# Hybrid Mamba-2 / feed-forward chain on one core: the sum over 1024 channels of the mixers' squares moves from TensorE (column-tiled products) to GpSimd (three additions)

## Chip, cores and metric

One Trainium2 chip, one NeuronCore of it. The metric is device time in microseconds (us) of one execution of the whole kernel, as the median of several runs. Everything is float32 (a few operands are rounded to fp32r). PE is TensorE, DVE is VectorE, ACT is ScalarE, POOL is GpSimd, SP is the sync engine, which here only issues DMAs.

## The reference, cut to what matters

Four layers one after the other over x of shape (4, 1024, 512): mixer A, feed-forward, mixer B, the same feed-forward again, each as x = x + layer(layernorm(x)). Both mixers are state-space mixers of width 1024: they project the token, convolve it, run the recurrence over time, and end with a gated normalisation over the 1024 channels:

```
mixer A:  yf  = y * silu(gate)
          var = mean(yf * yf, axis=-1)
          out = (norm_w * (yf * rsqrt(var + EPS))) @ out_proj_w.T
mixer B:  var = mean(square(y), axis=-1)
          out = ((y * rsqrt(var + EPS)) * norm_w * silu(z)) @ out_proj_w
```

What the change touches is the mean of the squares over the 1024 channels of each token.

## The kernel before

The 4096 tokens go through each mixer in 16 supertiles of 256 tokens, each of two tiles of 128 tokens (j = 0 and 1). Supertile 0, the last two and the 13 between them (a hardware loop) have the same body. The work of a supertile is software-pipelined: while supertile i is in its recurrence, TensorE projects supertile i+1 into the gaps ("fill"). The order on every engine is written out by hand, and semaphores connect the engines.

TensorE runs the list that `schedule(prev, nxt)` gives. Names of it that the text uses:

- `zza`, `zzb`, `z0a`, `z0b`, `z1`, `z2`, `blk..`, `dt`: projections of fill, line 655 (`dt` is line 684);
- `xT0..3`, `BT`/`GT` (`BG` in mixer A): transposes and small products at the head of a supertile;
- `yoffJa`, `yoffJb`: state times C, two banks for tile J (lines 725 and 727); `from_state` on DVE (line 1221) multiplies each by the decay into y1, in two halves, and GpSimd adds `skip` to y1 (line 1441);
- `segJ.p`: exponents of the decay matrices, from which ACT makes `decay` (lines 936 and 943) and DVE multiplies it by the masked product (`slot_mult`, line 1232) for the `ydiag` products;
- `rs0` and `prs` (line 746): the squares of a tile, summed. `rs0` is that of tile j=0, in the middle of its own supertile; `prs` is that of tile j=1, in the head of the next supertile;
- `rt0` and `prt` (line 750), then `out0` and `pout` (line 756): the turned column of sums, and the output product of the tile, which waits in TensorE's order behind `rt0`/`prt`;
- `small1` (line 716) follows `pout` by two uses; it takes over the PSUM bank of `pout`, which DVE's `out_add` (line 1277) has to have read.

All steps except `seg`, `ydiag`, `ident` and `xT` are "uses" of two PSUM banks in turn (`work`): a use may start when the use two before it has been read out (`freed`). With `rs0` and `prs` in the list, `yoff1a` takes the bank of `z0b`, `yoff1b` that of `rs0`, `rt0` that of `yoff1a`, and `out0` that of `yoff1b`.

The squares: DVE's `gate` (line 1257) writes yz = y * silu(z) in two halves; ACT's `square` (line 953) writes `sq`, [128 channels, 8 blocks, 128 tokens], in two halves. Mixer B squares y itself. `rs0`/`prs` multiplies each of the eight blocks by 32 columns of ones; block b goes to the column group b mod 4 of the array, so that four run side by side, and the bank then holds four partial sums, each repeated over 32 partitions. DVE copies it to `rs` (`square_sums`, line 1263), and `rt0`/`prt` multiplies `rs` by `quad_row`, which picks one partition of each group and adds them with the token turned to the partition. DVE makes the variance of it (line 1267), ACT its logarithm and exponential, DVE one Newton step, and `out_add` scales the output product and adds the residual.

DVE's order in the second half of a supertile of mixer B is: last state addition, `gate` of tile 0, the six multiply-adds of the last two convolution blocks (line 1111), `square_sums`, `from_state(1)`, `rms_var`, `slot_mult` of tile 1. In mixer A the convolution lies before the gate. In the head it is: masked product (1182), `make_xdt(0)` (1160 in B in two halves, 1165 in A), `square_sums`, `from_state(0)`, `rms_var`, `make_xdt(1)`, `slot_mult(0, 0)`, Newton step, `slot_mult(0, 1)`, `out_add`.

GpSimd's order of a tile (`tile_steps`) is: the second right side of the exponents (line 1406, B only), e (1421, j=0 only), `skip` (1435), y1 + skip (1441), xw (1448 in B in two halves, 1452 in A), state decay (1458).

Of the kernel before, what the change touches and what calls it, by code (L numbers as in the profile page):

```python
# [8 lines left out]
ALU = mybir.AluOpType  # L9
ACT = mybir.ActivationFunctionType  # L10

P = 128
# [16 lines left out]
FREE = 2  # L29
# [168 lines left out]
def build_constants(nc, ctx, ffn_w, mixers, weights, arena, mixer_signals, x_src):  # L198
# [18 lines left out]

    c["quad_row"] = sb("quad_row", [P, 1])
    hd = sb("hd", [P, 2, 4, 16])
# [13 lines left out]
    with nc.Block() as block:  # L233
# [44 lines left out]
        @block.vector  # L278
        def _(dve):
            dve.wait_ge(made, c["steps"])  # L280
            nc.vector.tensor_reduce(c["of_head"][:], hd[:].rearrange("p o e c -> p (o e) c"), mybir.AxisListType.X, ALU.add).then_inc(built, 1)
            nc.vector.tensor_reduce(c["low_row"][:], low[:].rearrange("p a b -> p (a b)"), mybir.AxisListType.X, ALU.add
                                    ).then_inc(built, 1)
            nc.vector.tensor_reduce(c["l_row"][:], lrow[:].rearrange("p a b -> p (a b)"), mybir.AxisListType.X, ALU.add
                                    ).then_inc(built, 1)
            nc.vector.tensor_reduce(c["quad_row"][:], c["ident"][:].rearrange("p (q e) -> p e q", e=32)[:, 0:1, :],
                                    mybir.AxisListType.X, ALU.add).then_inc(built, 1)
            dve.wait_ge(built, 4)
            nc.vector.tensor_scalar(c["sign_row"][:], c["low_row"][:], -2.0, 1.0, ALU.mult, ALU.add).then_inc(built, 1)
            nc.vector.tensor_scalar(c["s_row"][:], c["l_row"][:], -1.0, 1.0, ALU.mult, ALU.add).then_inc(built, 1)  # L290
            dve.wait_ge(built, 6)
            count = [6]
# [10 lines left out]
def mixer_phase(nc, sig, before, cfg, c, arena, later, psum, x_src, x_dst, w):  # L303
# [21 lines left out]
    with ctx:  # L325
# [100 lines left out]
        sq_done = sig("sq_done")  # L426
        rs_ready = sig("rs_ready")
        rv_ready = sig("rv_ready")
        r1_ready = sig("r1_ready")
# [20 lines left out]
        def head(prev, nxt):  # L450
            return (["zza", "xT0", "xT1", "xT2", "xT3"] + b_and_g + ["zzb"]
                    + (["prs"] if prev else []) + ["yoff0a", "yoff0b", "seg0.0"] + (["prt"] if prev else [])
                    + (["xnT0"] if nxt else []) + (["pout"] if prev else []) + (["xnT1"] if nxt else [])
                    + ["ident0", "small1"])

        def schedule(prev, nxt):
# [9 lines left out]
            steps += ["z0a", "z0b"] if nxt else []  # L466
            steps += ["rs0", "yoff1a", "yoff1b", "seg1.0", "rt0", "out0"]
            for p in range(NP):
# [29 lines left out]
        pro_steps = ["xnT0", "xnT1", "dt"] + blocks + ["z0a", "z0b", "z1", "z2", "sums", "small0"]  # L498
        epi_steps = ["prs", "prt", "pout"]
        first_uses, loop_uses, last_uses = ([s for s in schedule(*a) if is_use(s)]  # L500
# [43 lines left out]
        def freed(eng, name, i, n):  # L544
# [27 lines left out]
            elif name[:5] == "state":  # L572
                eng.wait_ge(state_ready, FREE + i * 4 + 2 * int(name[5]) + (2 if FOLD else "ab".index(name[6]) + 1))
            elif name in ("rs0", "prs"):
                eng.wait_ge(rs_ready, FREE + i * 2 + (name == "rs0"))
            elif name in ("rt0", "prt"):
                eng.wait_ge(rv_ready, FREE + i * 2 + (name == "rt0"))
            elif name in ("out0", "pout"):
                eng.wait_ge(out_done, FREE + i * 2 + (name == "out0"))
            else:  # L580
                raise ValueError(name)

        with nc.Block() as block:
# [68 lines left out]
            def _(pe):  # L652
# [12 lines left out]
                def use(name, sec):  # L665
# [63 lines left out]
                    elif name[:5] == "state":  # L729
# [11 lines left out]
                    elif name in ("rs0", "prs"):  # L741

                        pe.wait_ge(sq_done, FREE + 2 * (2 * i + (name == "rs0")))
                        for b in range(KE):
                            q = b % 4
                            mm = nc.tensor.matmul(bank[32 * q:32 * q + 32, 0:P], ones[:, 0:32], sq[:, b, :],
                                                  start=(b < 4), stop=(b >= 4))
                    elif name in ("rt0", "prt"):
                        pe.wait_ge(rs_ready, FREE + 2 * i + (name == "rt0"))
                        mm = nc.tensor.matmul(bank[:, 0:1], rs[:], c["quad_row"][:], start=True, stop=True)  # L750
                    else:
# [310 lines left out]
            def _(dve):  # L1062
# [197 lines left out]

                def square_sums(sec, name):
                    dve.wait_ge(work_full, sec.full(name))
                    nc.vector.tensor_copy(rs[:], sec.bank(name)[:, 0:P]).then_inc(rs_ready, 1)

# [23 lines left out]
                def supertile(sec, prev, nxt):  # L1288
                    i = sec.i
                    masked_gt(sec)  # L1290
                    make_xdt(sec, 0)
                    if prev:
                        square_sums(sec, "prs")
                    from_state(sec, 0)
# [31 lines left out]
                    square_sums(sec, "rs0")  # L1326
                    from_state(sec, 1)
# [25 lines left out]
                for s in (xn_ready, raw_ready, conv_done, halo_done, xdt_done, hilo_ready, y1_ready, state_ready,  # L1353
                          yz_done, out_done, rs_ready, rv_ready, m_ready):
                    dve.sem_inc(s, FREE)
# [38 lines left out]
                sec = epilogue()  # L1394
                square_sums(sec, "prs")
                rms_var(sec, "prt")
# [5 lines left out]
            def _(pool):  # L1402
# [10 lines left out]

                def tile_steps(i, j, ln=None):
                    tile = 2 * i + j
# [3 lines left out]
                    if j == 0:  # L1419
# [5 lines left out]
                        if FOLD:  # L1425

                            pool.wait_ge(dec_done, FREE + tile)
                            for q in range(2):
# [3 lines left out]
                            ins.then_inc(folded, 1)  # L1432
                            pool.wait_ge(folded, FREE + i + 1)
                    pool.wait_ge(xt_ready, FREE + 4 * i + 2 * j + 2)
                    nc.gpsimd.tensor_tensor(skip[:].rearrange("p (h q) -> p h q", h=H),
                                            xt[:, j, :].rearrange("p (h q) -> p h q", h=H),
                                            d_skip[:].unsqueeze(2).to_broadcast([P, H, HP]), ALU.mult
                                            ).then_inc(skip_done, 1)
                    pool.wait_ge(y1_ready, FREE + 2 * tile + 2)
                    pool.wait_ge(skip_done, FREE + tile + 1)  # L1440
# [22 lines left out]

                for s in (skip_done, y1x_ready, dec_done, kept, xw_ready, folded):
# [3 lines left out]
                tile_steps(0, 0)  # L1468
                tile_steps(0, 1, ln=2)
# [3 lines left out]
                for i in (NSUP - 2, NSUP - 1):  # L1473
                    tile_steps(i, 0)
                    tile_steps(i, 1)

def ffn_phase(nc, sig, before, tag, c, arena, following, psum, x_src, x_dst, w):
# [647 lines left out]
```

## Time and profile before

| | |
|---|---|
| median of 3 runs | 2862.99 us (2861.88 to 2865.03) |
| span of the profiled execution | 2859.7 us |
| granted TensorE clock, mean | 0.980 of full speed |
| PE busy | 2733.3 us, 96% |
| DVE busy | 2009.9 us, 70% |
| ACT busy | 1527.0 us, 53% |
| POOL busy | 926.1 us, 32% |
| supertile of mixer A | about 66.5 us |
| supertile of mixer B | about 78.7 us |

The profiled execution's own time is its span; the median of the runs lies 3.3 us (0.1%) above it. Times in rows are microseconds from the start of the span. A row of the timeline gives start, length, engine, line, operation, what is written and read; "x2" is a merged pair, and what stands in brackets is how long the engine sat idle before it and what ended that. Each float32 matrix product shows as two records.

### The profile page before, as it was taken

Reading aid. Unit: us, or ns where it says so; the run is one execution under the profiler, and the core shown is the slowest. Engines: PE = TensorE matmul, PEld = TensorE weight load, DVE = VectorE, ACT = ScalarE, POOL = GpSimd, SP = SyncE. Lnnn points to the kernel's source line nnn. Section 1 sums busy time; section 2 is a strip of 40 time slices with the busy share of each in tenths; the row PEclk is TensorE's granted clock in tenths of the full one; section 3 lists DMA queues with packets and bytes.
Section 4 is the critical chain, followed back from the end, with each engine's and each line's share of the span. In section 5 each row is a group of like instructions: output and inputs, shape, how many; then the busy total and the mean of one; then the engine's idle time right before and its main releaser. Section 6 shows DMA issues by size and latency. Waiting matters only on the chain. (4 is left out here: it accounts for less than half of the span.)

```text
span 2859.7 us, 49906 instructions
## 1 busy us (share of the span) xinstructions
PE 2733.3 (96%) x17464; PEld 1845.0 (65%) x17464; DVE 2009.9 (70%) x3695; ACT 1527.0 (53%) x2418; POOL 926.1 (32%) x614
## 2 busy tenths in 40 slices
PE   7999999999999999996899999999999999997996
PEld 6777766777766665455666666666666666664453
DVE  5666666666666663377788888888888888885267
ACT  3444444445455442341577666766667776665242
POOL 2222223222223321232233444333333334332134
PEclk9999999999999999998999999999999999998998
DMA  4000000000000034145000000000000000022333
GB/s 125 23 23 22 22 22 22 23 28 29 22 22 22 16 121 152 45 147 204 12 23 22 22 22 16 21 22 22 15 15 22 22 22 22 15 95 89 112 118 133
DMA packets 79935, 139.59 MB, mean 49 GB/s; under 512 B 17896, under 2 KB 17896, under 8 KB 78832
## 3 DMA queue, kind: packets, MB, share of 16 engines
q1 hardware_dynamic: 70752, 125.92, 12.9%
q10 hardware_dynamic: 9104, 12.63, 1.4%
q8 instruction: 48, 0.79, 0.1%
q14 instruction: 31, 0.25, 0.0%
HBM read 104.98 MB, written 33.55 MB: 48 GB/s over the span
## 5 line engine op out<-in xcount | busy, mean ns | idle before, releaser
L655 PE MATMUL work<-b_xnT,shared_w 128*128 128x256 f32 x2304 | 545.8, 388 | 1.8 <-DVE b_parts L1192 1.3
L655 PE MATMUL work<-a_xnT,shared_w 128*128 128x256 f32 x2176 | 509.4, 392 | 1.3
L655 PEld LDWEIGHTS work<-b_xnT,shared_w 128*128 128x128 f32 x2304 | 426.1, 191 | 90.6 <-issue 30.1
L655 PEld LDWEIGHTS work<-a_xnT,shared_w 128*128 128x128 f32 x2176 | 419.0, 195 | 73.8 <-issue 12.3
L1232 DVE TENSOR_TENSOR b_decay<-b_decay,b_gt 128x1024 f32<-128x1024 f32 x256 | 351.7, 1395 | 119.3 <-ACT b_decay L943 115.8
L936 ACT ACTIVATE b_decay<-seg 128x1024 f32<-128x1024 f32 x256 | 248.5, 1029 | 112.0 <-PE seg L781 111.8
L943 ACT ACTIVATE b_decay<-b_decay 128x1024 f32<-128x1024 f32 x256 | 266.1, 1073 | 0.0
L1406 POOL TENSOR_TENSOR b_rhs<-b_l_side,of_head 128x1024 fp32r<-128x1024 f32 x32 | 82.0, 2563 | 552.4 <-DVE b_l_side L1201 552.4
L1441 POOL TENSOR_TENSOR a_y<-a_y,a_skip 128x1024 f32<-128x1024 f32 x32 | 90.9, 2840 | 484.1 <-DVE a_y L1221 484.1
L1111 DVE SCALAR_TENSOR_TENSOR shared_cv<-shared_pre,a_conv_w,shared_cv 128x256 f32<-128x256 f32 x432 | 189.7, 482 | 74.6 <-ACT shared_cv L880 68.9
L1111 DVE SCALAR_TENSOR_TENSOR shared_cv<-shared_pre,b_conv_w,shared_cv 128x256 f32<-128x256 f32 x480 | 232.1, 517 | 14.2 <-ACT shared_cv L880 6.3
L756 PE MATMUL work<-a_w_out,a_yz 128*128 128x512 f32 x512 | 229.0, 600 | 2.3 <-DVE a_y L1221 0.5
L756 PE MATMUL work<-b_w_out,b_yz 128*128 128x512 f32 x512 | 226.8, 596 | 0.6
L879 ACT COPY shared_pre<-work 128x256 f32<-128x256 f32 x304 | 114.7, 377 | 201.4 <-PE work L655 201.2
L886 ACT COPY shared_z<-work 128x256 f32<-128x256 f32 (+1 forms) x192 | 85.8, 447 | 253.3 <-PE work L655 252.4
L1232 DVE TENSOR_TENSOR a_decay<-a_decay,a_gt 128x1024 f32<-128x1024 f32 x64 | 136.5, 2152 | 84.9 <-ACT a_decay L943 84.4
L756 PEld LDWEIGHTS work<-a_w_out,a_yz 128*128 128x128 f32 x512 | 95.5, 192 | 112.2 <-issue 108.5
L756 PEld LDWEIGHTS work<-b_w_out,b_yz 128*128 128x128 f32 x512 | 94.7, 190 | 109.1 <-issue 107.1
L795 PE MATMUL y<-b_decay,b_xdt 128*32 128x128 f32 x4096 | 142.8, 280 | 5.8 <-DVE b_decay L1232 5.7
L795 PEld LDWEIGHTS y<-b_decay,b_xdt 128*32 128x32 f32 x4096 | 105.6, 111 | 61.7 <-issue 50.8
L1441 POOL TENSOR_TENSOR b_y<-b_y,b_skip 128x1024 f32<-128x1024 f32 x32 | 82.9, 2591 | 130.6 <-DVE b_y L1221 130.6
L1653 PE MATMUL y<-f_x1T,shared_pre 128*128 128x512 f32 x256 | 122.9, 610 | 0.0
(314 smaller groups left out, 4612.4 us busy)
## 6 DMA issues: line engine op xcount, KB each, us to landing
shared_x<-in_L_attn_a_x SPq DMA_DIRECT2D x16, 512.0 KB, 3.5
a_x_res<-in_L_attn_a_x SPq DMA_DIRECT2D x32, 256.0 KB, 2.6
x_mid<-a_x_res SPq DMA_DIRECT2D x32, 256.0 KB, 2.1
shared_w<-in_L_ffn_d_w SPq DMA_DIRECT2D x2, 4096.0 KB, 14.0
f_d_w<-in_L_ffn_d_w SPq DMA_DIRECT2D x2, 4096.0 KB, 14.5
f_x_res<-x_mid SPq DMA_DIRECT2D x8, 1024.0 KB, 5.9
f_bc_w<-x_mid SPq DMA_DIRECT2D x8, 1024.0 KB, 5.6
shared_x<-x_mid SPq DMA_DIRECT2D x16, 512.0 KB, 3.6
```

What stands on the lines that cost most here:

```text
L655: mm = nc.tensor.matmul(dst, w_in[:, k, col:col + m], xnT[:, k, :], start=(k == 0), stop=(k == KD - 1))
L756: mm = nc.tensor.matmul(bank[:, :], yz[:, k, :], w_out[:, k, :], start=(k == 0), stop=(k == KE - 1))
L795: mm = nc.tensor.matmul(ybank[32 * q:32 * q + 32, slot * P:(slot + 1) * P], xdt[:, j, 4 * slot + q, 16 * odd:16 * odd + 32], decay[:, slot ...
L879: nc.scalar.copy(pre[0:m, b, HALO:], bank[0:m, 0:SUP])
L886: nc.scalar.copy(z_raw[:, got[0]:got[-1] + 1, :], sec.bank(name)[:, 0:len(got) * SUP].rearrange("p (b t) -> p b t", t=SUP)).then_inc(z_rea ...
L936: nc.scalar.activation(decay[:, slot_buffer(j, s)].rearrange("p h l -> p (h l)"), seg[s % 2][:, :], ACT.Relu, scale=-1.0).then_inc(seg_tak ...
L943: nc.scalar.activation(d, d, ACT.Exp, scale=-1.0).then_inc(exp_done, 1)
L1111: ins = nc.vector.scalar_tensor_tensor(out=cv[0:m, b, :], in0=pre[0:m, b, t:t + SUP], scalar=conv_w[0:m, b, t:t + 1], in1=cv[0:m, b, :], o ...
L1232: nc.vector.tensor_tensor(d, d, gt[:, j].unsqueeze(1).to_broadcast([P, 8, P]), ALU.mult).then_inc(m_ready, 1)
L1406: nc.gpsimd.tensor_tensor(rhs[1][:], l_side[:, 1].unsqueeze(1).to_broadcast([P, 8, P]), c["of_head"][:].unsqueeze(2).to_broadcast([P, 8, P ...
L1441: nc.gpsimd.tensor_tensor(y1[:], y1[:], skip[:], ALU.add).then_inc(y1x_ready, 1)
L1653: mm = nc.tensor.matmul(ybank[:, (m % 2) * 512:(m % 2 + 1) * 512], gate_w[:, k, m * P:(m + 1) * P], x1T[n][:, k, :], start=(k == 0), stop= ...
```

## The change

`rs0` and `prs` leave TensorE's list and with them two of the uses of the `work` banks; DVE's copy and `quad_row` go. GpSimd adds the eight blocks of `sq` in place: 512 columns, 256 columns, then 128 columns into `rs`. `rt0`/`prt` multiplies `rs` (now [128 channels, 128 tokens]) by one column of ones. On GpSimd the sums of the previous tile stand ahead of `skip` when j=0 (after e), and after `skip` and ahead of y1 + skip when j=1; those of the very last tile stand at the end.

```
-                    + (["prs"] if prev else []) + ["yoff0a", "yoff0b", "seg0.0"] + (["prt"] if prev else [])
+                    + ["yoff0a", "yoff0b", "seg0.0"] + (["prt"] if prev else [])
...
-            steps += ["rs0", "yoff1a", "yoff1b", "seg1.0", "rt0", "out0"]
+            steps += ["yoff1a", "yoff1b", "seg1.0", "rt0", "out0"]
...
-                    elif name in ("rs0", "prs"):
-
-                        pe.wait_ge(sq_done, FREE + 2 * (2 * i + (name == "rs0")))
-                        for b in range(KE):
-                            q = b % 4
-                            mm = nc.tensor.matmul(bank[32 * q:32 * q + 32, 0:P], ones[:, 0:32], sq[:, b, :],
-                                                  start=(b < 4), stop=(b >= 4))
                     elif name in ("rt0", "prt"):
                         pe.wait_ge(rs_ready, FREE + 2 * i + (name == "rt0"))
-                        mm = nc.tensor.matmul(bank[:, 0:1], rs[:], c["quad_row"][:], start=True, stop=True)
+                        mm = nc.tensor.matmul(bank[:, 0:1], rs[:], ones[:, 0:1], start=True, stop=True)
...
-                def square_sums(sec, name):
-                    dve.wait_ge(work_full, sec.full(name))
-                    nc.vector.tensor_copy(rs[:], sec.bank(name)[:, 0:P]).then_inc(rs_ready, 1)
...
+                def square_sums(tile):
+
+                    pool.wait_ge(sq_done, FREE + 2 * tile + 2)
+                    nc.gpsimd.tensor_tensor(sq[:, 0:4, :], sq[:, 0:4, :], sq[:, 4:8, :], ALU.add).then_inc(sq_halved, 1)
+                    pool.wait_ge(sq_halved, FREE + tile + 1)
+                    nc.gpsimd.tensor_tensor(sq[:, 0:2, :], sq[:, 0:2, :], sq[:, 2:4, :], ALU.add).then_inc(sq_quartered, 1)
+                    pool.wait_ge(sq_quartered, FREE + tile + 1)
+                    pool.wait_ge(rv_ready, FREE + tile)
+                    nc.gpsimd.tensor_tensor(rs[:], sq[:, 0, :], sq[:, 1, :], ALU.add).then_inc(rs_ready, 1)
...
+                    if j == 0 and sums_before:
+                        square_sums(tile - 1)
                     pool.wait_ge(xt_ready, FREE + 4 * i + 2 * j + 2)
...
+                    if j == 1:
+                        square_sums(tile - 1)
                     pool.wait_ge(y1_ready, FREE + 2 * tile + 2)
```

## Rows read from the trace of the kernel before

**Rows 1.** The page: its span line and the engines' busy time.

```profile
span 2859.7 us, 49906 instructions
...
PE 2733.3 (96%) x17464; PEld 1845.0 (65%) x17464; DVE 2009.9 (70%) x3695; ACT 1527.0 (53%) x2418; POOL 926.1 (32%) x614
```

**Rows 2.** Groups by line and form: busy us, mean ns, idle before.

```profile
L746 PE MATMUL work<-a_sq,ones 128*32 128x128 f32 x512 | 20.6, 279 | 3.8 <-ACT a_sq L953 3.8
L746 PE MATMUL work<-b_sq,ones 128*32 128x128 f32 x512 | 20.6, 279 | 5.7 <-ACT b_sq L953 5.7
```

**Rows 3.** One line's instructions each: min/median/max ns.

```profile
L1441 POOL TENSOR_TENSOR b_y<-b_y,b_skip x32: 2350/2366/2919, 1382.2 to 2596.9; 128x1024 f32<-128x1024 f32 x32
...
L2027 POOL TENSOR_TENSOR f_bc_w<-f_bc_w,f_out_beta_row x32: 1259/1267/1297, 1203.3 to 2850.9; 128x512 f32<-128x512 f32 x32
...
L1111 DVE SCALAR_TENSOR_TENSOR shared_cv<-shared_pre,b_conv_w,shared_cv x480: 470/482/1619, 1346.6 to 2528.3; 128x256 f32<-128x256 f32 x160
```

**Rows 4.** Timeline of mixer B around rs0, all engines.

```profile
2051.14 1.93 POOL L1435 TENSOR_TENSOR b_skip<-b_xt,b_d_skip 128x1024 f32<-128x1024 f32 x1
2051.25 1.19 ACT L953 ACTIVATE b_sq<-y 128x512 f32<-128x512 f32 x2 [2.90 <-DVE b_yz L1257]
2051.74 3.84 DVE L1111 SCALAR_TENSOR_TENSOR shared_cv<-shared_pre,b_conv_w,shared_cv 128x256 f32<-128x256 f32 x6
...
2054.12 0.65 PE L746 MATMUL work<-b_sq,ones 128*32 128x128 f32 x16
...
2054.70 2.27 PE L727 MATMUL work<-b_state,b_bcs 128*128 128x512 f32 x4
2055.50 0.28 DVE L1263 COPY b_rs<-work 128x128 f32<-128x128 f32 x1
...
2057.00 0.69 DVE L1221 TENSOR_TENSOR b_y<-work,b_e 128x512 f32<-128x512 f32 x1 [0.45 <-PE work L727]
...
2057.74 7.13 PE L756 MATMUL work<-b_w_out,b_yz 128*128 128x512 f32 x16
```

**Rows 5.** Timeline of mixer B, GpSimd and DVE at once.

```profile
2061.20 2.05 POOL L1448 TENSOR_TENSOR b_xw<-b_xdt,b_e 128x512 f32<-128x512 f32 x1
2060.35 1.97 DVE L1232 TENSOR_TENSOR b_decay<-b_decay,b_gt 128x1024 f32<-128x1024 f32 x1 [2.44 <-ACT b_decay L943]
```

**Rows 6.** Timeline of the head of a supertile of mixer B.

```profile
2007.95 1.09 ACT L953 ACTIVATE b_sq<-y 128x512 f32<-128x512 f32 x2
...
2008.34 1.94 POOL L1435 TENSOR_TENSOR b_skip<-b_xt,b_d_skip 128x1024 f32<-128x1024 f32 x1 [0.17 <-POOL b_e L1421]
2008.59 2.83 DVE L1160 TENSOR_TENSOR b_xdt<-b_xt,b_dt 128x512 f32<-128x512 f32 x2
...
2013.17 0.38 PE L750 MATMUL work<-quad_row,b_rs 128*128 128x1 f32 x2
...
2021.22 0.75 DVE L1277 SCALAR_TENSOR_TENSOR b_x_res<-work,b_rr,b_x_res 128x512 f32<-128x512 f32 x1
...
2022.33 0.61 PE L716 MATMUL work<-tri_le,b_aa 128*128 128x128 f32 x4
```

**Rows 7.** Timeline of mixer A: its head, then around rs0.

```profile
787.18 1.15 ACT L953 ACTIVATE a_sq<-a_yz 128x512 f32<-128x512 f32 x2
...
791.25 0.38 PE L750 MATMUL work<-quad_row,a_rs 128*128 128x1 f32 x2
...
800.85 0.44 PE L716 MATMUL work<-tri_le,a_aa 128*64 128x128 f32 x4 [0.15 <-DVE a_x_res L1277]
...
823.38 1.23 ACT L953 ACTIVATE a_sq<-a_yz 128x512 f32<-128x512 f32 x2 [3.69 <-DVE a_yz L1257]
...
828.23 7.13 PE L756 MATMUL work<-a_w_out,a_yz 128*128 128x512 f32 x16
```

**Rows 8.** Timeline of the end of mixer B.

```profile
2619.07 1.19 ACT L953 ACTIVATE b_sq<-y 128x512 f32<-128x512 f32 x2 [3.28 <-DVE b_yz L1257]
...
2621.55 0.35 PE L750 MATMUL work<-quad_row,b_rs 128*128 128x1 f32 x2 [0.49 <-DVE b_rs L1263]
```

More of the change, by code:

```diff
@@ L216, in build_constants @@
     c["keep"] = sb("keep", [P, NSUP + 1])
-    c["quad_row"] = sb("quad_row", [P, 1])
     hd = sb("hd", [P, 2, 4, 16])
@@ L285, in _ @@
                                     ).then_inc(built, 1)
-            nc.vector.tensor_reduce(c["quad_row"][:], c["ident"][:].rearrange("p (q e) -> p e q", e=32)[:, 0:1, :],
-                                    mybir.AxisListType.X, ALU.add).then_inc(built, 1)
-            dve.wait_ge(built, 4)
+            dve.wait_ge(built, 3)
             nc.vector.tensor_scalar(c["sign_row"][:], c["low_row"][:], -2.0, 1.0, ALU.mult, ALU.add).then_inc(built, 1)
             nc.vector.tensor_scalar(c["s_row"][:], c["l_row"][:], -1.0, 1.0, ALU.mult, ALU.add).then_inc(built, 1)
-            dve.wait_ge(built, 6)
-            count = [6]
+            dve.wait_ge(built, 5)
+            count = [5]
             def link(ins):
@@ L427, in mixer_phase @@
         rs_ready = sig("rs_ready")
+        sq_halved, sq_quartered = sig("sq_halved"), sig("sq_quartered")
         rv_ready = sig("rv_ready")
@@ L498, in mixer_phase @@
         pro_steps = ["xnT0", "xnT1", "dt"] + blocks + ["z0a", "z0b", "z1", "z2", "sums", "small0"]
-        epi_steps = ["prs", "prt", "pout"]
+        epi_steps = ["prt", "pout"]
         first_uses, loop_uses, last_uses = ([s for s in schedule(*a) if is_use(s)]
@@ L573, in freed @@
                 eng.wait_ge(state_ready, FREE + i * 4 + 2 * int(name[5]) + (2 if FOLD else "ab".index(name[6]) + 1))
-            elif name in ("rs0", "prs"):
-                eng.wait_ge(rs_ready, FREE + i * 2 + (name == "rs0"))
             elif name in ("rt0", "prt"):
@@ L740, in use @@
                                                   start=True, stop=True)
-                    elif name in ("rs0", "prs"):
-                        pe.wait_ge(sq_done, FREE + 2 * (2 * i + (name == "rs0")))
-                        for b in range(KE):
-                            q = b % 4
-                            mm = nc.tensor.matmul(bank[32 * q:32 * q + 32, 0:P], ones[:, 0:32], sq[:, b, :],
-                                                  start=(b < 4), stop=(b >= 4))
                     elif name in ("rt0", "prt"):
                         pe.wait_ge(rs_ready, FREE + 2 * i + (name == "rt0"))
-                        mm = nc.tensor.matmul(bank[:, 0:1], rs[:], c["quad_row"][:], start=True, stop=True)
+                        mm = nc.tensor.matmul(bank[:, 0:1], rs[:], ones[:, 0:1], start=True, stop=True)
                     else:
@@ L1291, in supertile @@
                     make_xdt(sec, 0)
-                    if prev:
-                        square_sums(sec, "prs")
                     from_state(sec, 0)
@@ L1325, in supertile @@
                         gate(sec, 0)
-                    square_sums(sec, "rs0")
                     from_state(sec, 1)
@@ L1353, in _ @@
                 for s in (xn_ready, raw_ready, conv_done, halo_done, xdt_done, hilo_ready, y1_ready, state_ready,
-                          yz_done, out_done, rs_ready, rv_ready, m_ready):
+                          yz_done, out_done, rv_ready, m_ready):
                     dve.sem_inc(s, FREE)
@@ L1394, in _ @@
                 sec = epilogue()
-                square_sums(sec, "prs")
                 rms_var(sec, "prt")
@@ L1412, in norm_rsqrt, with tile_steps @@
                     nc.gpsimd.tensor_tensor(ln_r[:], ln_v[:], c["root"][:], ALU.pow).then_inc(r0_ready, 1)
-                def tile_steps(i, j, ln=None):
+                def square_sums(tile):
[6 more added lines that the diff above has]
+                    nc.gpsimd.tensor_tensor(rs[:], sq[:, 0, :], sq[:, 1, :], ALU.add).then_inc(rs_ready, 1)
+                def tile_steps(i, j, ln=None, sums_before=True):
                     tile = 2 * i + j
@@ L1462, in tile_steps @@
                         norm_rsqrt(ln)
-                for s in (skip_done, y1x_ready, dec_done, kept, xw_ready, folded):
+                for s in (skip_done, y1x_ready, dec_done, kept, xw_ready, folded, rs_ready, sq_halved, sq_quartered):
                     pool.sem_inc(s, FREE)
@@ L1467, in _ @@
                 pool.wait_ge(small_loaded, 16 * 5)
-                tile_steps(0, 0)
+                tile_steps(0, 0, sums_before=False)
                 tile_steps(0, 1, ln=2)
@@ L1475, in _ @@
                     tile_steps(i, 1)
+                square_sums(2 * NSUP - 1)
 def ffn_phase(nc, sig, before, tag, c, arena, following, psum, x_src, x_dst, w):
```

## Prediction, made before the changed kernel was run

> **What bounds the kernel now.** I read the page first. PE is busy 96% of the span, DVE 70%, POOL 32% [rows 1]; the reader is to see that TensorE sets the pace and that GpSimd looks free. Next the groups by line: the work that leaves TensorE is 20.6 us in each mixer, 41.2 us in all, 1.4% of the span [rows 2]. A share says nothing of where a wait ends, so the rest comes from the timeline around the four places at which a tile's sum is made: `prs` in the head and `rs0` in the middle, in mixer A and in mixer B. There the question is what releases `out0`, and what releases `small1` after `pout`, since TensorE is dense behind both and a shift of either moves the whole supertile. In the middle of mixer B DVE is already the late one: the squares are summed by 2054.77, but DVE's copy starts only at 2055.50, when its six convolution steps are through; the second half of y1 ends at 2057.69 and `out0` starts at 2057.74 [rows 4]. In the head, `small1` starts at 2022.33 in mixer B, behind an `out_add` that ended at 2021.97 [rows 6], and at 800.85 in mixer A, where it waited for `out_add` [rows 7]. So DVE is the second bound, close behind, at three of the four places.
>
> **Price of the three sums.** GpSimd's add of two full tiles takes 2350 ns for 1024 columns and 1259 ns for 512 [rows 3]: (2350 - 1259) / 512 = 2.13 ns a column on a base of 0.17 us. So 512, 256 and 128 columns take 1.26, 0.71 and 0.44 us, 2.41 us; with about 0.08 us for each hand-over, `rs` is there 2.65 us after the squares if nothing is in the way. Columns 256 and 128 are not in the trace; below they are bounded by nothing and by one 512-column add each (3.8 us in all).
>
> **What they cost DVE.** In the head of mixer B, two halves of xdt take 2.83 us beside a `skip` of 1.94 us [rows 6], and one half alone takes about 0.68 us in the same line's shortest case, so DVE stood for nearly the whole of `skip`. In the middle, six convolution steps take 3.84 us, with `skip` on until 2053.07, where six at 0.42 us of spacing need 2.5 us [rows 4]; one such step is 470 ns alone and up to 1619 [rows 3]. The other way round, xw at 2061.20 takes 2.05 us, double its need, because the decay product that started at 2060.35 runs to 2062.32; and when that ends the waiting GpSimd goes first [rows 5]. I read this as: a DVE instruction that reads two tiles of SBUF and a GpSimd instruction exclude each other, and they take turns. What reads PSUM on DVE (`from_state`, the gate, `out_add`) isn't held up (0.69 us each time [rows 4]). Of a GpSimd instruction all but some 0.15 us at each end holds, so three sums hold about 2.41 - 0.45 = 1.95 us.
>
> The Trainium skill says the same of the pair (page "SBUF — State Buffer", section "SBUF: two separate sides"): it is an exclusive lock, kept for the whole instruction, and the other fully blocks; the trace agrees with [rows 5]. A sharing of bandwidth would leave most of the 1.95 us to DVE, and by it the change would come out as the first rival below.
>
> **Middle of mixer B (15 supertiles with convolution behind the gate).** Removed: `rs0` (0.65 us of PE) and the copy (0.28 us of DVE). Squares end at 2052.44, `skip` at 2053.07 [rows 4]. The sums then take turns with the convolution steps (first sum up to about 2054.5, then a step, second to 2055.4, a step, third to 2056.2), and the six steps end near 2055.5 + 1.95 = 2057.5 instead of 2055.5. Then two halves of y1, 1.29 us: 2058.8. `out0` needs the bank of `yoff1b`, so it starts at about 2058.85 instead of 2057.74: **+1.1 us**. `rt0` waits for the first half (2058.2), not for `rs`. Behind: y1 + skip on GpSimd is 1.1 us late too, and has 5 us before `ident1`. Bounds: if GpSimd lets the convolution run through first, sums lie from 2055.5 to 2058.0 and `out0` goes at 2058.5 (+0.75); if the sums hold DVE for all of 2.65 us, +1.8. I take +1.1, as the turns in [rows 5] give it. Sum 15 x 1.1 = 16.5.
>
> **Head of mixer B (15).** Squares end at 2009.04 [rows 6]. One half of xdt(0) gets between the sums, so `rs` comes at 2012.0 to 2012.3 and `prt` at about 2012.3, 0.85 us earlier than 2013.17. But `skip` now stands behind the sums: it runs from 2012.3 to 2014.2, where DVE wants xdt(1) from 2012.9. In turns: half of xdt(1) to 2014.8, y1 + skip to 2017.0, the other half to 2017.6, half of xw to 2018.5, `slot_mult(0,0)` to 2019.7, half of xw to 2020.6, `slot_mult(0,1)` to 2021.7, `out_add` to 2022.4 instead of 2021.97. `small1` then starts near 2022.6 instead of 2022.33: **+0.3**. TensorE's gain at `prt` is lost at `small1`. Bounds: -0.8 (no blocking, everything follows `prt`) and +0.9 (one more turn lost). ACT isn't moved: its table load and gate function stand before the exponentials. 15 x 0.3 = 4.5.
>
> **Head of mixer A (15).** Squares end at 788.33; xdt(0) on DVE (1.2 us, from 787.66) holds the first sum until 788.87; `rs` at 791.3, `prt` at 791.35 against 791.25 [rows 7], so no gain. `skip` again moves behind the sums, to 793.2, and xdt(1), which ran at 791.77 with nothing beside it, waits for it. In the same turns `out_add` ends at 801.3 instead of 800.80, and `small1`, at 800.85 already released by it [rows 7], follows: **+0.5**, bounds -0.2 and +0.9. 15 x 0.5 = 7.5.
>
> **Middle of mixer A (15).** The convolution is done before the gate, so nothing on DVE takes turns. Squares end at 824.61 [rows 7], `rs` comes at 827.3, `rt0` at 827.35, `out0` 0.49 us later at 827.85 instead of 828.23: **-0.4**, bounds -0.6 (the y1 halves decide, 827.6) and +0.75 (sums of 3.8 us). 15 x -0.4 = -6.
>
> **Ends.** Behind the last tile nothing covers the chain. From the end of the squares at 2620.26 to `prt` at 2621.55 are 1.29 us [rows 8]; with the sums 2.65, so +1.4 in each mixer, +2.8. `quad_row` is one small reduction ahead of everything: nothing. The waits that are added stand on GpSimd; what is queued behind them is `skip` in the head, priced above, and y1 + skip in the middle. No DMA is issued or moved; the SP queue's store of x_res only follows `out_add`.
>
> Sum: 16.5 + 4.5 + 7.5 - 6 + 2.8 = +25.3 us on the profiled execution's 2859.7 us, 2885 us. The median of the runs lies 3.3 us above that execution, so **2888 us**, 0.9% slower.
>
> **Rivals.** (1) *Hidden, faster.* The sums don't hold DVE. Then `out0` in the middle of B goes at 2056.9 (-0.85), the head of B gains 0.8, A's head 0.15 and middle 0.4: 15 x 2.2 = 33 less 2.8 gives about **2833 us**. For it: GpSimd is idle two thirds of the time and TensorE is the bound [rows 1]. Against it: xdt and convolution beside `skip`. It decides once the sums take less than about 0.8 us from DVE in the middle of B.
> (2) *The two sides cancel.* TensorE's savings are the size of DVE's losses: `small1` is held up nowhere in B (gain 0.8 instead of 0.3 lost), the rest as forecast: 25.3 - 16.5 = +9, and with -0.2 in A's head 0: about **2863 us**.
> (3) *Worse cascade.* Each head loses a further turn (+0.9 twice) and the middle of B 1.8 us, A's middle gains nothing: 15 x 3.6 + 2.8 = +57: **2920 us**. For it: the exchange at the lock in [rows 5] is read from few cases.
> Beside (1): TensorE's array changes its grouping for `rs0` and back. The Trainium skill (page "TensorEngine Tiling (Array Packing)", section "Tiling Modes") says that such a change drains TensorE; no row here shows the drain by itself, and it would come back at both ends of each removed step.
>
> **How the numbers follow.** Forecast 0.66, of which nothing ends below 2869; (1) 0.13, (2) 0.11, (3) 0.10. What this kernel's measurement can tell from no change is about 0.2%, 5.7 us. Faster 0.15 (all of (1), a little of (2)); same 0.08; slower 0.77. The likeliest case has 2873 to 2905 for itself: 2859.7 + 3.3 plus the sum with the middle of B at its low bound of +0.75 and the heads at 0 (+10), and with each head a little over half way to its upper bound (+42). The range 2858 to 2918 leaves out (1) and the upper half of (3).
>
> **What the profile after would show.** Right: six convolution steps behind the gate of B take about 4.4 to 5.8 us; the wait of TensorE before `rt0`/`out0` in B is ended by DVE's y1, and `out0` starts about 6.4 us after the end of the squares (5.3 before); xdt(1) in the heads starts later than `prt` and is long; line 750 waits for GpSimd's `rs` in A. Supertile of B +1.4 us, of A +0.1 us. Wrong: conv steps at 470 ns beside the sums; a supertile of B shorter than before; GpSimd's adds of 256 and 128 columns above 1 us each, which would turn A's middle into a loss. The weakest step is the order in which the two engines get the lock, and with it both heads.

## The result and the profile after

The changed kernel takes 2878.65 us (median of 4 runs, 2876.51 to 2879.03) where the kernel before takes 2863.17 us (4 runs, 2861.88 to 2865.03): a ratio of 1.0052, 95% interval 1.0038 to 1.0066. It is 0.5% slower. The direction is as forecast; the size is 9 us below the 2888 us of the forecast.

The page of the changed kernel, its span and busy line and three groups (busy us, mean ns; idle before them and its releaser):

```profile
span 2877.3 us, 47876 instructions
...
PE 2700.9 (94%) x16440; PEld 1830.6 (64%) x16440; DVE 2054.4 (71%) x3630; ACT 1527.0 (53%) x2418; POOL 1095.4 (38%) x806
...
L1100 DVE SCALAR_TENSOR_TENSOR shared_cv<-shared_pre,b_conv_w,shared_cv 128x256 f32<-128x256 f32 x480 | 255.4, 565 | 14.2 <-ACT shared_cv L869 6.3
L745 PE MATMUL work<-b_w_out,b_yz 128*128 128x512 f32 x512 | 240.7, 626 | 3.2 <-DVE b_y L1210 3.2
```

TensorE has 32 us less to do than in [rows 1] and the span is 17.6 us longer. GpSimd took on 169 us. DVE lost 64 copies (18 us) and is still 44 us busier. Work that the diff doesn't touch takes longer: the convolution of mixer B 23 us (517 ns a step before, 565 after), xdt 23 us and the decay products 15 us over both mixers. The output products of B are untouched too, and their mean is 626 ns instead of 596.

The three sums by line (min/median/max ns, first and last start):

```profile
L1399 POOL TENSOR_TENSOR a_sq<-a_sq x32: 1262/1266/1596, 93.1 to 1085.0; 128x512 f32<-128x512 f32 x32
...
L1399 POOL TENSOR_TENSOR b_sq<-b_sq x32: 1258/1442/1692, 1420.8 to 2633.2; 128x512 f32<-128x512 f32 x32
...
L1401 POOL TENSOR_TENSOR a_sq<-a_sq x32: 722/727/740, 94.4 to 1086.3; 128x256 f32<-128x256 f32 x32
...
L1404 POOL TENSOR_TENSOR a_rs<-a_sq x32: 453/458/462, 95.2 to 1087.1; 128x128 f32<-128x128 f32 x32
```

At their shortest they cost 1.26, 0.72 and 0.45 us, as worked out from [rows 3]. In mixer B the median of the first is 0.18 us more: in the middle of B it runs beside the convolution.

The middle of mixer B, timeline of all engines (the supertile of [rows 4], 7.55 us later):

```profile
2058.50 1.93 POOL L1429 TENSOR_TENSOR b_skip<-b_xt,b_d_skip 128x1024 f32<-128x1024 f32 x1
2058.61 1.20 ACT L942 ACTIVATE b_sq<-y 128x512 f32<-128x512 f32 x2 [2.90 <-DVE b_yz L1246]
2059.10 5.39 DVE L1100 SCALAR_TENSOR_TENSOR shared_cv<-shared_pre,b_conv_w,shared_cv 128x256 f32<-128x256 f32 x6
...
2060.39 1.45 POOL L1399 TENSOR_TENSOR b_sq<-b_sq 128x512 f32<-128x512 f32 x1
...
2060.64 1.48 DVE L1100 SCALAR_TENSOR_TENSOR shared_cv<-shared_pre,b_conv_w,shared_cv 128x256 f32<-128x256 f32 x1
...
2061.92 0.78 POOL L1401 TENSOR_TENSOR b_sq<-b_sq 128x256 f32<-128x256 f32 x1
...
2062.16 0.83 DVE L1100 SCALAR_TENSOR_TENSOR shared_cv<-shared_pre,b_conv_w,shared_cv 128x256 f32<-128x256 f32 x1
...
2062.78 0.52 POOL L1404 TENSOR_TENSOR b_rs<-b_sq 128x128 f32<-128x128 f32 x1
...
2062.91 0.67 DVE L1100 SCALAR_TENSOR_TENSOR shared_cv<-shared_pre,b_conv_w,shared_cv 128x256 f32<-128x256 f32 x1
...
2064.41 1.28 DVE L1210 TENSOR_TENSOR b_y<-work,b_e 128x512 f32<-128x512 f32 x2
...
2065.15 0.38 PE L739 MATMUL work<-ones,b_rs 128*128 128x1 f32 x2 [1.45 <-DVE b_y L1210]
...
2065.74 7.13 PE L745 MATMUL work<-b_w_out,b_yz 128*128 128x512 f32 x16 [0.22 <-DVE b_y L1210]
```

Six convolution steps take 5.39 us instead of 3.84 us. The three rows of single steps (x1) are the second, third and fourth of the six, each from a narrower window of the same timeline. The three sums end at 2061.84, 2062.70 and 2063.30, and these steps end at 2062.12, 2062.99 and 2063.58: each step that met a sum ends 0.28 to 0.29 us behind it, whatever its own start, where a step alone takes 0.48 us. That is what turns give. If the two only shared a bandwidth, a slowed step could also end ahead of the sum beside it, and none does. `rs` is complete at 2063.30, but `rt0` starts at 2065.15, behind the first half of y1 on DVE, and `out0` behind the second half. TensorE stands for 1.45 + 0.22 us: `rs0`, which used to fill 0.65 us of this stretch, is gone, and DVE is later.

The head of mixer B, the same supertile (against [rows 6]):

```profile
2019.58 1.94 POOL L1429 TENSOR_TENSOR b_skip<-b_xt,b_d_skip 128x1024 f32<-128x1024 f32 x1
2019.73 0.38 PE L739 MATMUL work<-ones,b_rs 128*128 128x1 f32 x2
2020.24 4.59 DVE L1149 TENSOR_TENSOR b_xdt<-b_xt,b_dt 128x512 f32<-128x512 f32 x2
...
2028.80 0.74 DVE L1263 SCALAR_TENSOR_TENSOR b_x_res<-work,b_rr,b_x_res 128x512 f32<-128x512 f32 x1
2029.59 0.71 PE L712 MATMUL work<-tri_le,b_aa 128*128 128x128 f32 x4 [0.54 <-DVE b_x_res L1263]
```

Mixer A, head and then middle of one supertile (against [rows 7], 3.75 us earlier):

```profile
787.64 1.90 POOL L1429 TENSOR_TENSOR a_skip<-a_xt,a_d_skip 128x1024 f32<-128x1024 f32 x1
787.73 0.38 PE L739 MATMUL work<-ones,a_rs 128*128 128x1 f32 x2 [0.68 <-POOL a_rs L1404]
...
797.48 0.44 PE L712 MATMUL work<-tri_le,a_aa 128*64 128x128 f32 x4 [0.68 <-DVE a_x_res L1263]
...
823.46 0.46 POOL L1404 TENSOR_TENSOR a_rs<-a_sq 128x128 f32<-128x128 f32 x1
...
824.28 7.13 PE L745 MATMUL work<-a_w_out,a_yz 128*128 128x512 f32 x16
```

In both heads `skip` stands behind the sums, xdt(1) is long (4.59 us for its two halves in B, 3.46 us before), and `small1` waits for `out_add`. In the middle of A nothing is lost.

**Where the 17.6 us are.** From the starts of successive supertiles (the activation of xs) in both traces. Mixer A: 15 periods average 66.48 us before and 66.04 after. Behind a shorter first one they come in two lengths, 65.79 and 67.47 before (7 each), 65.6 (9) and 67.27 (5) after. Mixer B: 78.6 to 79.0 before, most of them 78.65, but for a last one of 79.85; after, nine of 79.1 and six of 80.8 to 81.0, mean 79.80. So a usual supertile of A is 0.2 us shorter, one of B 0.46 us longer; besides, 1.7 us come and go by the piece, six times more in B and two times fewer in A. Up to the last store of A the changed kernel is 2.8 us ahead (loop -6.6, its last supertile with the epilogue +3.5, the start the rest). B costs 20.2 us (loop +15.8, last supertile +4.4).

**The piece of 1.7 us.** Windows of 4 us of the changed kernel: a short supertile of A, a long one of A, a long one of B (length; PE, PEld, DVE, ACT, POOL busy with instructions; granted clock; DMA share, GB/s):

```profile
133.00:137.00 4.00, 3.34 (x31) 2.93 (x30) 2.49 (x4) 0.59 (x1) 3.81 (x3) 1.00 0.17 66
137.00:141.00 4.00, 4.00 (x21) 3.54 (x21) 1.14 (x6) 1.55 (x5) 0.00 (x0) 1.00 0.22 66
...
264.00:268.00 4.00, 3.33 (x32) 2.92 (x30) 2.66 (x4) 0.59 (x1) 3.92 (x3) 1.00 0.17 66
268.00:272.00 4.00, 4.00 (x15) 3.30 (x15) 1.14 (x6) 1.13 (x4) 0.07 (x1) 0.62 0.24 66
...
1742.00:1746.00 4.00, 2.34 (x11) 0.91 (x9) 3.90 (x8) 2.22 (x4) 1.35 (x3) 1.00 0.00 0
1746.00:1750.00 4.00, 4.00 (x6) 1.77 (x7) 3.13 (x2) 2.08 (x4) 3.93 (x2) 0.62 0.00 0
```

One window of the kernel before, in a long supertile of A:

```profile
203.00:207.00 4.00, 4.00 (x12) 3.21 (x12) 0.89 (x5) 1.30 (x4) 0.00 (x0) 0.57 0.28 66
```

PE's timeline in that supertile of B:

```profile
1745.36 0.38 PE L739 MATMUL work<-ones,b_rs 128*128 128x1 f32 x2 [1.44 <-DVE b_y L1210]
...
1745.96 8.83 PE L745 MATMUL work<-b_w_out,b_yz 128*128 128x512 f32 x16 [0.21 <-DVE b_y L1210]
```

After a stand of 1.44 + 0.21 us the clock is granted at 0.62 of full speed over 4 us, most of that time at the lower of its two levels (1.2 instead of 2.4 GHz), and `out0` takes 8.83 us instead of 7.13. The stretch at the lower level lasts 3.4 us (granted 0.50 from 1746.94 to 1750.35), and half of it is the 1.7 us. The same stand at 2065 left it at 7.13 us. In A the fall comes just behind `small1`, in 5 of 15 supertiles; the two shown have the same busy time of PE ahead of it to 0.01 us (3.34 and 3.33), and one falls. The kernel before had it too, in 7 supertiles of A at the same place (0.57 in the window above; that supertile began at 179.05), with a stand of 0.15 us there [rows 7]; I had averaged over it as "about 66.5 us". There the falls come in every second supertile, 133.1 us apart. The first supertile of each mixer, whose work isn't dense yet, has a stretch at the lower level in every kernel here, the one before too; the counts leave it out.

The end of mixer B, timeline (against [rows 8]):

```profile
2631.87 1.30 ACT L942 ACTIVATE b_sq<-y 128x512 f32<-128x512 f32 x2 [3.94 <-DVE b_yz L1246]
...
2635.98 0.56 PE L739 MATMUL work<-ones,b_rs 128*128 128x1 f32 x2 [4.22 <-POOL b_rs L1404]
2636.40 9.51 PE L745 MATMUL work<-b_w_out,b_yz 128*128 128x512 f32 x16
```

TensorE stands for 4.22 us where [rows 8] show 0.49, because `prs` no longer breaks the wait, and then does `pout` in 9.51 us instead of 7.11 (in A 8.81 instead of 7.11).

### The profile page after: what moved, and what is told of

The parts are those of the page before. It is cut to its first block and busy times, and to the rows that moved or that the text cites. A ratio compares the mean times of both kernels' runs of the same rounds, so it can differ in the third digit from the quotient of the medians.

```text
span 2877.3 us, 47876 instructions
## 1 busy us (share of the span) xinstructions
PE 2700.9 (94%) x16440; PEld 1830.6 (64%) x16440; DVE 2054.4 (71%) x3630; ACT 1527.0 (53%) x2418; POOL 1095.4 (38%) x806
## 5 line engine op out<-in xcount | busy, mean ns | idle before, releaser
L1221 DVE TENSOR_TENSOR b_decay<-b_decay,b_gt 128x1024 f32<-128x1024 f32 x256 | 361.3, 1433 | 94.8 <-ACT b_decay L932 91.4
L1100 DVE SCALAR_TENSOR_TENSOR shared_cv<-shared_pre,b_conv_w,shared_cv 128x256 f32<-128x256 f32 x480 | 255.4, 565 | 14.2 <-ACT shared_cv L869 6.3
L745 PE MATMUL work<-b_w_out,b_yz 128*128 128x512 f32 x512 | 240.7, 626 | 3.2 <-DVE b_y L1210 3.2
L1399 POOL TENSOR_TENSOR a_sq<-a_sq 128x512 f32<-128x512 f32 x32 | 45.1, 1409 | 487.2 <-ACT a_sq L942 487.2
L1394 POOL TENSOR_TENSOR ln_r<-ln_v,root 128x2 f32<-128x2 f32 x30 | 34.3, 1142 | 235.6 <-DVE ln_v L1065 235.6
```

What stands on the lines that cost most here:

```text
L745: mm = nc.tensor.matmul(bank[:, :], yz[:, k, :], w_out[:, k, :], start=(k == 0), stop=(k == KE - 1))
L1100: ins = nc.vector.scalar_tensor_tensor(out=cv[0:m, b, :], in0=pre[0:m, b, t:t + SUP], scalar=conv_w[0:m, b, t:t + 1], in1=cv[0:m, b, :], o ...
L1221: nc.vector.tensor_tensor(d, d, gt[:, j].unsqueeze(1).to_broadcast([P, 8, P]), ALU.mult).then_inc(m_ready, 1)
L1399: nc.gpsimd.tensor_tensor(sq[:, 0:4, :], sq[:, 0:4, :], sq[:, 4:8, :], ALU.add).then_inc(sq_halved, 1)
```

## The experiments

Each ran beside the kernel before on the same chip (its median 2863 to 2864.5 us).

**Sums that nobody uses.** The kernel before, with the three adds put into GpSimd's order at the change's places, into a spare tile. TensorE's and DVE's work stay as they were; ACT's next squares wait for the third add as well, and in the trace it was never the wait that held them (they waited for the gate alone).

```diff
+def ghost_sums(tile):        # gh is a spare tile
+    pool.wait_ge(sq_done, FREE + 2 * tile + 2)
+    nc.gpsimd.tensor_tensor(gh[:, 0:4, :], sq[:, 0:4, :], sq[:, 4:8, :], ALU.add).then_inc(gh_a, 1)
...
+                    if j == 0 and sums_before:
+                        ghost_sums(tile - 1)
...
+                    if j == 1:
+                        ghost_sums(tile - 1)
```

> The kernel before, with the three additions on GpSimd added at the places where the change has them, but into a spare tile that nobody on the path reads (only the next tile's squares wait for them). TensorE and DVE do all that they did. Theory L (the additions cost by excluding DVE's two-input instructions): the six convolution steps behind the gate of mixer B take about 5.4 us instead of 3.84, out0 in B is about 1.3 us later, both heads lose 0 to 0.4 us, so 2863 + 20 to 35 us. Rival W (the loss of the changed kernel is the longer wait of TensorE for rs, and GpSimd's additions disturb nobody): 2863 us within 3, convolution 3.84 us.

Measured 2900.54 us, ratio 1.0129 (1.0112 to 1.0146). The expected range of theory L ended at 2898. Its timeline in the middle of B:

```profile
2074.31 5.41 DVE L1114 SCALAR_TENSOR_TENSOR shared_cv<-shared_pre,b_conv_w,shared_cv 128x256 f32<-128x256 f32 x6
2075.61 1.45 POOL L1419 TENSOR_TENSOR b_gh<-b_sq 128x512 f32<-128x512 f32 x1
...
2079.98 1.13 PE L729 MATMUL work<-b_state,b_bcs 128*128 128x512 f32 x2 [1.58 <-DVE b_rs L1266]
```

The adds alone, feeding nothing, stretch the six steps from 3.84 to 5.41 us and cost 37 us. About 8.5 us of that are the clock: five long supertiles more at 1.7 us each (nine long supertiles in A instead of seven, three in B instead of none). A usual supertile of A is 0.3 us longer, one of B 1.36 us. In B the loss is larger than in the changed kernel because DVE's copy, behind the stretched steps, now holds up `yoff1b`: TensorE stands 1.58 us for it. GpSimd's work isn't free although GpSimd has time; the changed kernel, which has the same adds and does without the products and the copy, is 22 us faster than this one.

The Trainium skill says so of the pair (page "SBUF — State Buffer", section "SBUF: two separate sides"): a GpSimd instruction and a DVE instruction with two inputs in SBUF exclude each other, and whichever is first holds the other off for the whole instruction. The trace agrees: 5.41 us here, and the ends of the single steps in the changed kernel.

**One sum instead of three.** The changed kernel with the 128-column add only; blocks 2 to 7 are left out of the variance.

```diff
-nc.gpsimd.tensor_tensor(sq[:, 0:4, :], sq[:, 0:4, :], sq[:, 4:8, :], ALU.add).then_inc(sq_halved, 1)
...
-nc.gpsimd.tensor_tensor(sq[:, 0:2, :], sq[:, 0:2, :], sq[:, 2:4, :], ALU.add).then_inc(sq_quartered, 1)
```

> The changed kernel with one addition of 128 columns instead of three (0.46 us of GpSimd instead of 2.45; blocks 2 to 7 are left out of the variance). Theory L: the convolution group is back near 4.2 us, TensorE's wait before rt0 in mixer B falls under 0.4 us, with it the phases at half clock in out0, and the saved column-tiled products show: about 2835 us. Rival (the gain isn't there in any case, because TensorE's removed steps were hidden behind DVE): 2855 to 2865 us.

Measured 2829.94 us, ratio 0.9886 (0.9869 to 0.9902). Nearly every period of A is 64.69 us, nearly every one of B 78.48; the six steps take 4.05 us, and TensorE no longer waits ahead of `rt0`. So the first two sums cost 49 us, and what the change removes is worth 33 us if most of the sums is gone. Both figures have the clock in them: one long supertile in A (seven before, five in the changed kernel) and two in B (none and six). The kernel comes within 4 us of the first rival's 2833 us, which had no term for the clock, so that nearness is in part luck.

**Work in TensorE's hole.** The changed kernel, with six products nobody uses behind `seg1.0` in B, once the squares are there.

```diff
+if name == "rt0" and cfg.tag == "b":
+    pe.wait_ge(yz_done, FREE + 2 * (2 * sec.i + 1))
+    pe.wait_ge(sq_done, FREE + 2 * (2 * sec.i + 1))
+    keep_running(nc, ybank, ident, 6)
```

> The changed kernel with six unused 128x128 float32 products (1.3 us) on TensorE in mixer B just ahead of rt0, where it waits 1.45 us for DVE's y1. Theory C (in 6 of 15 supertiles of B the wait lets the granted clock fall and out0 then takes 8.8 instead of 7.1 us): all supertiles of B take 79.1 us, none 80.8, and the kernel 2878.6 - 10 = about 2868 us. Rival (the longer supertiles come from something else, or the products only delay rt0): same or up to 5 us slower.

Measured 2864.75 us, ratio 1.0005 (0.9996 to 1.0015). PE's timeline:

```profile
2056.79 1.60 PE L54 MATMUL y<-ident 128*128 128x128 f32 x12
...
2058.92 7.13 PE L745 MATMUL work<-b_w_out,b_yz 128*128 128x512 f32 x16 [0.21 <-DVE b_y L1214]
```

`out0` starts no earlier, yet B's periods are all 79.1 to 79.4 us and the kernel is 13.9 us faster than the changed one: 10.1 us in B's loop and 3.3 in its last supertile with the epilogue. A, where nothing was filled, kept its five falls. That is the clock's share of the loss.

**Mixer A alone.** The change in A, mixer B as before.

```diff
+NEW = cfg.tag in "a"      # selects the form of every part of the change
```

> The change in mixer A alone; mixer B keeps its column-tiled sums on TensorE. By the two profiles mixer A had become 2.8 us shorter up to its last store and mixer B 20.2 us longer, so 2863 - 3 = 2860 us (2857 to 2863). If A and B influence each other through anything but the order in time (for instance the clock): up to 2866.

Measured 2861.87 us, ratio 0.9994 (0.9984 to 1.0004). A 66.01 us on average. B 78.96: most periods 78.65 as before, and a last one of 83.04, with a stretch at the lower clock in it. The 0.5% is lost in B.

**The convolution out of the sums' way.** The changed kernel, and in a second run the kernel before, with the last six convolution steps of B moved behind `rt0`'s reciprocal on DVE.

```diff
+late = blks if g + 1 == NS and NP > 1 else []
-for k in range(0, len(blks), 2):
+for k in range(0, len(blks) - len(late), 2):
...
 rms_var(sec, "rt0")
+if NP > 1 and late:
+    conv_blocks(sec, late)
```

> The changed kernel, with DVE's last six convolution steps of mixer B moved from before from_state(1) to behind rms_var of rt0, into the time in which DVE waits for the first exponential. Theory L (the additions matter because they stretch the convolution that stands in front of y1): out0 in B starts about 1.2 us earlier than in the changed kernel, TensorE's 1.45 us wait goes, no supertile of B has a phase at half clock: 2878.6 - 15 x 1.2 - 10 = about 2850 us. Rival W (rt0 waits for GpSimd's three additions in any case): out0 moves by less than 0.3 us, 2870 to 2879 us.

> The kernel before with the same move of the six convolution steps. It is the fair partner of the run above. By the timeline of before, DVE's copy comes 0.6 us earlier and y1 with it 0.3 to 0.5 us: 2863 - 15 x 0.4 = about 2857 us. If the move is what helps and not the sums, both fall alike, by 15 us or more.

Measured 2863.75 us (1.0005, 0.9996 to 1.0015) for the changed kernel, 2882.38 us (1.0069, 1.0050 to 1.0088) for the one before. Timeline of the changed kernel so moved, and of the one before so moved:

```profile
2053.49 7.13 PE L745 MATMUL work<-b_w_out,b_yz 128*128 128x512 f32 x16
2053.58 8.07 DVE L1100 SCALAR_TENSOR_TENSOR shared_cv<-shared_pre,b_conv_w,shared_cv 128x256 f32<-128x256 f32 x6
```

```profile
2067.78 8.06 DVE L1111 SCALAR_TENSOR_TENSOR shared_cv<-shared_pre,b_conv_w,shared_cv 128x256 f32<-128x256 f32 x6
```

Both expectations were missed (2850 and 2857 us), the second in its sign too. In the changed kernel so moved TensorE's hole ahead of `rt0` is gone and no supertile of B has a fall (78.87 us each), but the six steps now lie beside y1 + skip, xw and the state on GpSimd and take 8.07 us. The pair still answers the question: with the convolution away from the sums, the same change makes the kernel 19 us faster (2882.4 to 2863.8); with the convolution beside them, 15 us slower. In the loops of the two traces B gains 17.2 us (80.02 to 78.87 us on average, 79.82 to 78.87 in most) and A 7.1, as without the move; the last supertiles with their epilogues lose 6.5. The move by itself costs the kernel before 19 us, so the gain is against a slower partner, and no more than the sign of B's part should be taken from it.

**The order in the heads.** The changed kernel with the head's sums behind `skip`, in both mixers and in a second run in A alone (the condition then also asks for mixer A).

```diff
-if j == 0 and sums_before:
-    square_sums(tile - 1)
 pool.wait_ge(xt_ready, FREE + 4 * i + 2 * j + 2)
 ...
-if j == 1:
+if j == 1 or sums_before:
     square_sums(tile - 1)
```

> The changed kernel, with the sums of a j=0 step behind skip instead of ahead of it. In mixer A's head the additions end at the same time (the squares are late, skip is not), but skip no longer meets xdt(1), so small1 comes 0.7 us earlier: supertile of A 65.6 to about 64.9 us, 10 us in all. In B's head prt comes 0.8 us later and out_add about as before: 0. So 2878.6 - 10 = about 2868 us. If the heads are bound by TensorE and not by the order of the two engines at the lock: 2878 within 3 us.

> The changed kernel, with the j=0 sums behind skip in mixer A alone. Mixer A as in the run that had it in both (971.4 us for 15 periods instead of 990.6), mixer B as in the changed kernel (79.8 us): 2878.6 - 19 to 20 = about 2859 us. Rival (what the other run lost came from A's side too): 2870 us or more.

Measured 2885.96 us (1.0088, 1.0071 to 1.0105) in both mixers and 2857.15 us (0.9978, 0.9967 to 0.9989) in A alone. The first of them, timeline in the head of A and of B:

```profile
772.20 0.38 PE L739 MATMUL work<-ones,a_rs 128*128 128x1 f32 x2 [0.69 <-POOL a_rs L1404]
...
781.21 0.44 PE L712 MATMUL work<-tri_le,a_aa 128*64 128x128 f32 x4
...
2007.81 3.91 DVE L1149 TENSOR_TENSOR b_xdt<-b_xt,b_dt 128x512 f32<-128x512 f32 x2
...
2012.89 0.38 PE L739 MATMUL work<-ones,b_rs 128*128 128x1 f32 x2 [1.43 <-POOL b_rs L1404]
...
2023.07 0.71 PE L712 MATMUL work<-tri_le,b_aa 128*128 128x128 f32 x4 [1.10 <-DVE b_x_res L1263]
```

In A `small1` no longer waits, and behind the first supertile the clock never falls: 14 of 15 periods are 64.76 to 64.87 us, the mean is 64.76 instead of 66.04. Of these 1.28 us, some 0.73 are the shorter supertile (65.6 to 64.87), the rest the falls (5 x 1.68 / 15 = 0.56). In B the same order is bad: the sums and `skip` both delay xdt, `rs` comes later, TensorE waits 1.43 us and then 1.10 us, and the mean period is 81.85 us instead of 79.80. Every supertile of B now has a fall, 15 instead of six; a supertile with a fall in its middle takes 82.5 us, so without one about 80.8 (an estimate, less 1.7), against 79.1 in the changed kernel. Some 1.7 of the 2.05 us are thus the order itself and the rest the clock. I had expected B to stay as it was and got a loss of the kind of the third rival, by another order of turns.

**The order in the epilogue.** The changed kernel with the output product ahead of the ones product.

```diff
-epi_steps = ["prt", "pout"]
+epi_steps = ["pout", "prt"]
```

> The changed kernel, with pout ahead of prt in each mixer's epilogue, so that the last output product runs while GpSimd adds. TensorE then doesn't stand 4.2 us, its clock doesn't fall there, and the additions are covered; the Newton chain comes behind the product instead. The last squares to the last out_add took 9.5 us before and 12.7 and 14.0 us in the changed kernel; here about 9.7 in both: 2878.6 - 7 = about 2871.5 us. If the fall of the clock in the tail isn't due to the wait: 2875 to 2879 us.

Measured 2869.09 us, ratio 1.0029 (1.0017 to 1.0040). Timeline at the end of A:

```profile
1083.24 7.10 PE L745 MATMUL work<-a_w_out,a_yz 128*128 128x512 f32 x16 [0.89 <-DVE a_yz L1246]
...
1091.91 0.75 DVE L1263 SCALAR_TENSOR_TENSOR a_x_res<-work,a_rr,a_x_res 128x512 f32<-128x512 f32 x1
```

`pout` waits for the gate, not for the sums, and runs in 7.10 us; from the last squares to the end of `out_add` A takes 8.9 us instead of 12.7 (9.5 before the change), and B 9.2 instead of 14.0 (9.5). The sums are hidden behind the product.

**What the experiments point to.** The change in A only, with the head's sums behind `skip` and `pout` first in A's epilogue; mixer B as before.

```diff
-epi_steps = ([] if NEW else ["prs"]) + ["prt", "pout"]
+epi_steps = ["pout", "prt"] if NEW else ["prs", "prt", "pout"]
```

> Mixer A with the change, its j=0 sums behind skip and pout ahead of prt in its epilogue; mixer B as before, with the column-tiled sums. From the supertile times so far: mixer A's 15 periods 971.4 us (64.76 on average, no supertile with a phase at half clock) instead of 997.2, its tail about as before, mixer B as before: 2863 - 26 - 1 = 2836 us, 0.9% faster than before. Rival (A's gain depends on something that B's form brings with it, or the clock falls elsewhere): 2845 to 2860 us.

Measured 2831.69 us (2830.78 to 2832.49), ratio 0.9887 (0.9871 to 0.9904): 1.1% faster than the kernel before. Its page:

```profile
span 2829.6 us, 48861 instructions
...
PE 2700.0 (95%) x16952; PEld 1822.1 (64%) x16952; DVE 2017.7 (71%) x3663; ACT 1526.1 (54%) x2418; POOL 1009.5 (36%) x710
```

A averages 64.80 us with no fall behind its first supertile, B 78.75 as before. Of the 30 us between the two profiled spans, 25.3 are A's 15 periods.

## Why the prediction was right in direction, and where its numbers were off

- **The price of the sums** (1.26, 0.71, 0.44 us from two rows of another line) was right to 0.02 us.
- **What they cost DVE.** Right in kind, shown by the unused sums and by the ends of the single steps. Mis-sized: forecast 1.95 us on six convolution steps, measured 1.55.
- **Middle of B, +1.1 us:** measured +0.74 (`out0` 0.45 us later against the start of its supertile, of which the head had gained 0.29). That is the low bound of the step. Who goes next was read rightly: the sums went in between the steps, and y1 released `rt0` and `out0`. 11.1 us instead of 16.5.
- **Head of B, +0.3 us:** wrong in sign, and the step of the prediction that failed is the wait: it let `small1` follow `out_add`, then and now. `out_add` ends at 2021.99 in the scale of [rows 6], where 2021.97 stood, but `small1` had started only at 2022.33: it had stood behind other products of TensorE, not behind `out_add`. With `prs` gone those come earlier (`prt` by 1.0 us, 2012.18 against 2013.17 in that scale), `small1` waits for `out_add`, and it starts 0.29 us earlier. -4.4 us instead of +4.5.
- **Head of A, +0.5 us:** measured +0.38; the walk through the turns held to about 0.1 us (`out_add` forecast to end at 801.3, at 801.18 in the scale of [rows 7]). **Middle of A, -0.4 us:** measured -0.58. Together -3.0 us instead of +1.5.
- **Ends, +2.8 us:** measured +3.2 in A and +4.5 in B, 7.7 in all. The hand-over was right (2.81 us from squares to `prt` in B, forecast 2.65, before 1.29). What was missed is that TensorE stands 4.22 us there and runs `pout` at a lower clock.
- **The interval of the likeliest case** doesn't follow from its terms. The middle of B at +0.75 with the heads at 0 gives +8 us, not +10, and heads half way to their upper bounds give +33 to +36, not +42. That makes about 2871 to 2899 us instead of 2873 to 2905; the measured time lies in both.
- **The signs to look for:** the convolution (5.39 us), DVE's y1 as what ends TensorE's wait in B, the late and long xdt(1), and `rt0`/`prt` waiting for `rs` in A were all there. `out0` starts 5.9 us behind the end of the squares (forecast 6.4). Supertiles were off: B +0.46 us without falls and +1.05 on average (forecast +1.4), A -0.2 and -0.4 (forecast +0.1).
- **The term that was missing.** The sum had none for the granted clock. With `rs0` gone and DVE later there is a hole of 1.65 us in B, and in six supertiles a fall behind it: +10.1 us. Two falls fewer in A: -3.4 us.

Together 11.1 - 4.4 - 3.0 + 7.7 + 10.1 - 3.4 = +18.1, less 1.2 for the long last period of B before: +16.9 us of the 17.6 seen (0.7 us stays unassigned). So the lock's part was forecast too high (22.5 us in the four loop terms, 3.7 measured), and the clock's part, about 7 us in the loops and some 4 at the ends, was not in it. The two errors point opposite ways, so the nearness of 2888 to 2878.65 is in part luck. With B's falls filled in, the kernel stands at rival (2)'s 2863 us: 2864.75.

Of the **rivals**, (1) fell with the unused sums; its 2833 us was reached only where two of three sums were gone. (3) was not seen in the changed kernel, but its mechanism is real: the other order in B's head lost 2.05 us a supertile against it, clock included.

Left open: what decides in which supertiles the clock falls. The stand ahead of it is the same in those that fall and in those that don't, and in A it was 0.15 us before (seven falls) and 0.67 us after (five), while the run with one sum had 0.20 us there and one fall. So for B the filler shows that the hole is what the falls need; for A that `small1`'s wait is what they need is argued, from runs that have neither the wait nor the falls but are also shorter by the supertile.

Left open too: what the column-tiled products cost TensorE by the change of its grouping. No run here isolates it.

## What to carry to other kernels

Work moved to an idle GpSimd was paid by DVE here wherever DVE had two-input work from SBUF at that moment; price it by what DVE does beside it, place by place, and give the change only to the places that pay (here mixer A, not B). When a small product leaves TensorE, look at what it was covering: if the engine then stands there, the next long product may run at the lower clock (8.83 instead of 7.13 us here, in six of 15 supertiles). At an epilogue, put the product that doesn't need the sums ahead of the one that does.

## What the runs showed of the hardware that I had not expected

- Stands of TensorE of 0.15 to 0.7 us (A's `small1`) or 1.65 us (B's `rt0`) in a stretch that is otherwise dense are followed by a fall of the granted clock (0.57 to 0.62 over 4 us) in 5 to 7 of 15 supertiles, at 1.7 us each, and the same stand in the others by none. Six filler products in the hole of B removed all six there; in the three runs with an order without `small1`'s wait A had none.
- The same six convolution steps of 128x256 take 3.84, 5.4 or 8.07 us by what GpSimd does beside them (one `skip`; `skip` and three sums; y1 + skip, xw and the state).
- The order of `skip` and the sums on GpSimd, which don't depend on each other, is worth 1.28 us a supertile one way in A and 2.05 us the other way in B, the clock's part (about 0.6 and 0.3 us) included.
